# Softmax maxima in four double takes, and values in 256-query blocks behind every two pairs of products

## The reference, cut to what matters

```
scores  = einsum('blhd,bshd->bhls', q, k) / sqrt(16)
weights = softmax(scores, axis=-1)
out     = einsum('bhls,bshd->blhd', weights, v)
```

## Time and profile before

| | |
|---|---|
| device time, three runs | 3438.78, 3441.13, 3443.15 us; median 3441.13 us |
| span of the profiled execution | 3437.2 us (its own device time is not listed; the median is 3.9 us above this span) |
| TensorE busy | 3289.5 us, 96% of the span |
| VectorE busy | 2955.9 us, 86% |
| ScalarE busy | 2473.5 us, 72% |
| first to last score product, layer 0 and layer 1 | about 181 to 1405 us and 2196 to 3416 us |

### The profile page before, as it was taken

The page is one execution under the profiler, slowest core; times in us unless marked ns, Lnnn a source line. Parts: engine busy times, 40 slices in busy tenths (PEclk is TensorE's granted clock), DMA queues, the critical chain, the costliest instruction groups (busy, mean ns, idle before and its releaser), DMA issues. The chain is left out here.

```text
span 3437.2 us, 66173 instructions
## 1 busy us (share of the span) xinstructions
PE 3289.5 (96%) x25137; PEld 1521.3 (44%) x25138; DVE 2955.9 (86%) x4695; ACT 2473.5 (72%) x4700; POOL 580.5 (17%) x601
## 2 busy tenths in 40 slices
PE   8999999999999999888899889999999999999997
PEld 5433333333333333567677656533333333333332
DVE  8889999999999997353787665499999999999991
ACT  4178888888888888533333324688888888888886
POOL 4410000000000000053331143133333210000001
PEclk9689999999999999889999999999999999999999
DMA  8451220202021100345010376513132231202001
GB/s 270 138 140 47 41 39 15 44 16 39 15 44 32 24 15 5 129 135 191 27 36 12 121 248 200 139 35 58 35 52 45 52 64 27 44 16 40 15 16 49
DMA packets 306934, 232.77 MB, mean 68 GB/s; under 512 B 205591, under 2 KB 257720, under 8 KB 301970
## 3 DMA queue, kind: packets, MB, share of 16 engines
q1 hardware_dynamic: 290308, 179.45, 22.6%
q0 software_dynamic: 14832, 47.79, 4.3%
q10 hardware_dynamic: 1504, 1.64, 0.1%
HBM read 126.49 MB, written 102.76 MB: 67 GB/s over the span
## 5 line engine op out<-in xcount | busy, mean ns | idle before, releaser
L957 ACT ACTIVATE att_l_probs<-att_l_s_ps 128x512 f32<-128x512 f32 x4096 | 2142.0, 599 | 309.5 <-PE att_l_s_ps L900 269.3
L981 DVE TENSOR_REDUCE att_in_part_max<-att_l_max_ps 128x1 f32<-128x512 f32 (+1 forms) x2928 | 2292.0, 885 | 9.9 <-PE att_l_max_ps L890 9.5
L915 PE MATMUL att_l_o_ps<-att_l_probs,att_l_v_sb 128*17 128x512 f32 (+2 forms) x11776 | 1171.5, 470 | 1.4 <-DMA att_l_v_sb<-v_rows 1.1
L900 PE MATMUL att_l_s_ps<-att_in_q_sb,att_in_k_sb 50*128 50x512 f32 x2048 | 734.4, 453 | 10.1 <-DVE att_l_o_ps L995 9.0
L900 PE MATMUL att_l_s_ps<-att_in_q_sb,att_l_k_sb 50*128 50x512 f32 x2048 | 727.0, 453 | 1.3
L890 PE MATMUL att_l_max_ps<-att_l_k_sb,att_in_q_sb 50*128 50x512 f32 x2048 | 722.4, 445 | 5.2 <-DVE att_in_part_max L981 5.2
L890 PE MATMUL att_l_max_ps<-att_in_k_sb,att_in_q_sb 50*128 50x512 f32 x1856 | 660.0, 449 | 5.0 <-DVE att_in_part_max L981 4.8
L890 PEld LDWEIGHTS att_l_max_ps<-att_l_k_sb,att_in_q_sb 50*128 50x128 f32 x2048 | 336.2, 184 | 319.7 <-DVE att_in_part_max L981 297.8
L900 PEld LDWEIGHTS att_l_s_ps<-att_in_q_sb,att_l_k_sb 50*128 50x128 f32 x2048 | 328.6, 184 | 267.5 <-ACT att_l_probs L957 238.4
L900 PEld LDWEIGHTS att_l_s_ps<-att_in_q_sb,att_in_k_sb 50*128 50x128 f32 x2048 | 335.1, 186 | 241.3 <-ACT att_l_probs L957 202.3
L890 PEld LDWEIGHTS att_l_max_ps<-att_in_k_sb,att_in_q_sb 50*128 50x128 f32 x1856 | 307.8, 186 | 290.5 <-DVE att_in_part_max L981 268.4
(11 more groups left out here) (264 smaller groups left out, 2758.3 us busy)
## 6 DMA issues: line engine op xcount, KB each, us to landing
att_in_q_sb<-q_hi SPq DMA_DIRECT2D x256, 64.0 KB
slot_rows<-att_l_zeros POOLq DMA_DIRECT2D x10, 1024.0 KB, 4.5
ffn_parts<-slot_rows SPq DMA_DIRECT2D x40, 256.0 KB, 3.1
tile_out<-ffn_parts SPq DMA_DIRECT2D x40, 256.0 KB, 2.2
att_in_q_sb<-q_lo SPq DMA_DIRECT2D x128, 72.0 KB
att_l_v_sb<-v_rows SPq DMA_DIRECT2D x16, 544.0 KB, 15.2
att_in_k_sb<-k_hi SPq DMA_DIRECT2D x32, 256.0 KB, 8.9
att_l_k_sb<-k_hi SPq DMA_DIRECT2D x32, 256.0 KB, 9.4
```

Of the source, the lines that this page charges most:

```text
L900: nc.tensor.matmul(s_ps[:, c % SB], k_sb[j // GPB % 2][rows, pair, u * P:(u + 1) * P], q_sb[rows, j % QR, pair], start=True, stop=True).th ...
L915: last = nc.tensor.matmul(o_ps[32 * h:32 * h + AUG, c0:c1], v_sb[:, j // GPB % 2, u, h * AUG:(h + 1) * AUG], probs[:, (n * KT + u) % PB, h ...
L957: nc.scalar.activation(probs[:, (n * KT + u) % PB, h], s_ps[:, c % SB], ACT.Exp, scale=float(HD) ** -0.5).then_inc(exp_done, 1)
L981: nc.vector.reduce_max(dst, banks, AX.X).then_inc(units_taken, 1)
```

## The change

The takes become four doubles (units 0 and 1, 2 and 3, 4 and 5, 6 and 7). A double now covers one pair in each of two neighbouring units of the same product index, so the two columns of `part_max` it writes are neighbours too; the halves change places in `part_max`, and for that `first_maxima` writes its banks the other way round and `store_shift` reads the other half.

`ROUNDS` becomes four entries with two pairs each. After each two pairs follows a block of values with 256 columns: first the two blocks of the odd key tile before (`back` is 1), then the two of the even tile. The first period has its order within the same loop: two pairs, 256 columns of the last step's last tile, two pairs, its other 256 columns, four pairs, then all 512 columns of the new step's first tile.

```diff
-            last = nc.tensor.matmul(ps[:, k % 2 * 2 + half], ...
+            last = nc.tensor.matmul(ps[:, k % 2 * 2 + 1 - half], ...
...
-            eng.dma_start(dst, src[part:part + 1, half]).then_inc(ai.shift_stored, 16)
+            eng.dma_start(dst, src[part:part + 1, 1 - half]).then_inc(ai.shift_stored, 16)
...
-TAKES = ((0,), (1, 2), (3,), (4,), (5, 6), (7,))
+TAKES = ((0, 1), (2, 3), (4, 5), (6, 7))
...
-ROUNDS = ((3, 0, 288), (2, 288, 512), (3, 0, 512))
+ROUNDS = ((2, 1, 0, 256), (2, 1, 256, 512), (2, 0, 0, 256), (2, 0, 256, 512))
...
-                    if w == 0:
-                        products(n, w, 0, 3)
-                        if n > 0:
-                            values(n - 1, KT - 1, 0, G)
-                        products(n, w, 3, 5)
-                        values(n, 0, 0, G)
-                        continue
                     pair = 0
-                    for r, (count, c0, c1) in enumerate(ROUNDS):
+                    for count, back, c0, c1 in ROUNDS:
                         products(n, w, pair, count)
                         pair += count
-                        values(n, STEP_TILES * w - (r < 2), c0, c1)
+                        if w > 0:
+                            values(n, STEP_TILES * w - back, c0, c1)
+                        elif back and n > 0:
+                            values(n - 1, KT - 1, c0, c1)
+                        elif c1 == G and not back:
+                            values(n, 0, 0, G)
...
-                first = 2 * k + half
-                dst = part_max[:, g % 2, first:first + 1] if len(units) == 1 else part_max[:, g % 2, first:first + 4:3]
+                first = 2 * k + 1 - half
+                dst = part_max[:, g % 2, first:first + len(units)]
```

More of the change, by code:

```diff
@@ L256, in first_maxima @@
             rows = slice(half * HROWS, half * HROWS + XROWS)
-            last = nc.tensor.matmul(ps[:, k % 2 * 2 + half], ai.q[rows, j, pair, tile * P:(tile + 1) * P],
+            last = nc.tensor.matmul(ps[:, k % 2 * 2 + 1 - half], ai.q[rows, j, pair, tile * P:(tile + 1) * P],
                                     ai.k[0][rows, pair, part * G:(part + 1) * G], start=True, stop=True)
```

## The result

The changed kernel took 3507.8 us (median of 4 runs, 3504.3 to 3509.6) against 3440.0 us before (4 runs, 3438.5 to 3443.2): a ratio of 1.0194, with a 95% interval of 1.0179 to 1.0208. It is slower by 68 us; 3494 was forecast, in a range from 3455 to 3525. The profiled execution took 3508.3 us with a span of 3506.5 us, which is 69.3 us longer than the span before.

The account below looks back on a forecast made before the run. VectorE was taken to bound the kernel, TensorE 0.1 us per period behind. Steps growing from 38.15 to 39.14 us add 60 us over two layers, less 7 in the last periods: 3441 + 53 = 3494 us, range 3455 to 3525.

Parts of the forecast that it names:

- The bound before: Before the change VectorE's takes set the pace at 4.64 us per period, with TensorE at 4.55 without waits.
- the bound by 0.35 us per period: After the change TensorE, at 4.87 us per period, exceeds VectorE's 4.52 and sets the pace.
- The price of a trip: TensorE going once more from products to values and back: about 0.3 us, making a period 4.87 us.
- VectorE's gain: Four double takes replace six takes, saving 0.12 to 0.13 us per period, which only becomes idle time.
- The sign that I named for it: VectorE idle before its takes, about 0.35 us per period, ended by a maximum product; no gaps would mean wrong.
- The margin before the values: In the new order exponentials end at 1.72 us from a group's start, values ask at 1.875: 0.15 to spare.
- the rival of waiting exponentials: Values or banks wait in the new order, 0.1 us twice a period: 98 us more, 3592 us; chance 0.05.
- First period: Each step's first period, transpose included, goes from 5.20 to about 5.05 us; ends 4.55 and 5.20.
- tail: Last 12 periods, without maxima: 4.61 us falls to 4.3 as ScalarE starves less, gaining 7 us; ends 0 and 12.
- the draw: Rival: each of four groups costs 0.03 us less, period 4.76, tail gains; within 7 us of 3441; chance 0.03.
- The ends named for the block: TensorE's block of 256 value columns, taken as 0.555 us, could lie between 0.50 and 0.61.
- The rival with VectorE as the bound: Extra trips hide behind weight loads and VectorE still sets the pace: step 37.15 us, total 3373 us; chance 0.09.

## Why the prediction was right, step by step

**The bound before.** VectorE, as said: short takes alone bring 51 us. TensorE's distance to it came out at the size forecast, but by two errors that cancel. The forecast set 4.55 us of TensorE against 4.64 of takes. The old order comes down to 4.62 only, since it then waits for ScalarE; but the 1.0 us of transpose, reciprocal and row maxima in each step, left out of that comparison, are VectorE's work too. By the step it is 38.15 against 37.3 us, 0.8 or 0.10 a period: the number was right by luck. For the same reason "the bound by 0.35 us per period" is too much: with the forecast's own 37.15 us for VectorE it is (39.22 - 37.15)/8 = 0.26. None of this entered the sum, which goes from the measured 38.15 to the new period.

**The price of a trip.** Two pairs were put at 0.66 and 256 columns at 0.555; measured are 0.66 and 0.556, a period of 4.876 against 4.87. Three experiments bear on the cause: a fifth trip costs 0.32 more (0.3 was said), the width of blocks in three trips costs nothing, and six takes in place of four cost nothing in four trips. The traces also show where the 0.32 lies. Groups of one, two and three pairs take 0.43, 0.66 and 0.91 us (runs with one trip more, after, and short takes before; medians), 0.24 for each further pair, which leaves 0.19 for the group as such. Blocks of 128, 224, 256, 288 and 512 columns take 0.34, 0.50, 0.56, 0.61 and 0.98 and lie on one line, which leaves 0.13 at no columns. A trip is one more group and one more block: 0.19 + 0.13 = 0.32. The forecast had the same 0.3 as 0.2 and 0.1. That changing the tiling mode drains TensorE (the Trainium skill, TensorEngine Tiling (Array Packing), Key Properties) fits with these runs: products and columns stay the same while the number of mode changes grows. That the 0.32 us is this drain no run here shows, for each trip also brings four more matmuls of values. These may be the 0.13; the 0.19 comes without any more products.

**VectorE's gain.** Four doubles were said to save 0.12 us per period and to be worth nothing behind TensorE. Short takes in the changed kernel show the second half of it. The sign that I named for it did not come: I expected idle time before the takes and said I would be wrong without gaps, and the profile shows VectorE busy for 39.23 of 39.23 us. By its own words the forecast would have been given up for wrong; the sign was badly chosen. Records overlap when takes follow at 1.13, and stretching that to 1.21 closes the overlap and opens no gap. The spacing, the chain and the waits carry the proof.

**Waits inside the order.** The margin before the values was put at 0.15 us and is 0.25; the rival of waiting exponentials did not come, although a list of waits sorted by size suggests it.

**First period, tail.** The first period is 5.09 (5.05 forecast); a step 39.22 (39.14). It was 5.20 before, so the moved transpose, which stands in it, is not where the time is lost. The last periods gained less than forecast. ScalarE there:

```profile
1390.66 2.07 ACT L955 ACTIVATE att_l_probs<-att_l_s_ps 128x512 f32<-128x512 f32 x4 [0.15 <-PE att_l_s_ps L900]
1392.88 2.07 ACT L955 ACTIVATE att_l_probs<-att_l_s_ps 128x512 f32<-128x512 f32 x4 [0.15 <-PE att_l_s_ps L900]
```

Four exponentials in 2.22 make 4.44 a period; 4.3 was taken. The gain is 0.17 x 24 = 4 us and not 7.

**Where the missing 14 us are.** 3494 was forecast, 3507.8 measured. Of the sum, +53, the two layers show +63: 0.08 x 61 = 5 from the step, 3 from the tail, 2 from both layers' edges. Another 7 us are the middle, which no step of the prediction touched. Some 3 come off again: the profiled executions are 69.3 us apart and the medians 67.8, the sum started from a median of 3441.1 that is now 3440.0, and the rest of the program is 0.7 shorter.

**Slips in the working.** In the draw, 0.03 less in each of four groups of 1.215 makes 4.74, not 4.76. The ends named for the block, the first period and the last periods add up to 3438 to 3530; the stated 3455 to 3525 is narrower than their sum. Neither moved the forecast.

**The rival with VectorE as the bound** is out: with takes of half the length the changed kernel's time stays the same. The rule that TensorE's headroom is judged by the busy share of its weight loads (the Trainium skill, Perfetto Trace Analysis, Identifying the Most-Contended Engine) does not hold here: the share is 13.89 of 39.23 us, 35%, while TensorE sets the pace.

**Open.** Why the middle took 6.9 us longer. Stretches with a granted clock of 0.50 add up to 124.6 us there after the change and to 110.3 before; the repeated run has 120.5, and the kernel with the transpose one take later 113.7 with a middle as short as before. So a longer middle goes with more of it, though not strictly. What sets these stretches no run tells apart.

No experiment points to a version that beats both kernels: the old order was within 0.1 us per period of what TensorE and ScalarE allow it, even takes of half the length bring it to 3391 only, and each arrangement with other takes or trips was slower or equal.

## What to carry to other kernels

Where two engines look full, find the period of each alone before moving work from one to the other: saving 0.12 us per period on the engine that waits least is lost if the other one, 0.1 behind, gets one more switch between two kinds of matmul at 0.32. Count all that an engine does in a full round, the rare small operations too. A take over several banks must not span a block of other work on the producing engine, since the banks are held through it and the loop closes (5.66 us in place of 4.88). To see whether a busy engine is the bound, look at the spacing of its starts, or shorten its work and see whether the time moves.

## What the runs showed of the hardware that I had not expected

Merging two takes of 512 columns saves little: 2 x 0.595 - 1.13 = 0.06 us. And a stall can cost more than its length. In the run with six takes inside their groups, TensorE stood idle for 1.05 us in a step's first period, and from 2681.0 on it was busy throughout at a granted clock of 0.50, which is 1.2 GHz:

```profile
2680.28 0.50 PE L890 MATMUL att_l_max_ps<-att_in_k_sb,att_in_q_sb 50*128 50x512 f32 x2 [1.05 <-DVE att_in_part_max L979]
```

```profile
2681.00:2684.40 3.40, 3.40 (x21) 0.74 (x20) 2.31 (x5) 1.33 (x3) 1.00 (x1) 0.50 0.09 18
```

Its two attentions hold 14 such stretches, 51 us in all, and each begins 2.0 to 2.6 us behind the start of the transpose that VectorE had waited for; the run with the transpose one take later has none at these places. All that its attentions run at 0.50 adds up to 75.9 us, against 30.7 in that other run. Half of the 45 us more, an estimate that goes by TensorE being busy throughout the stretch shown, is 23 us. With the 61 us of the longer first periods and a middle that is 5 us longer (793.8 against 789.0) this makes 89 of the 93 us between the two runs. Why these first periods were followed by such a stretch and the others were not, no run tells.
